# Buffers of a cross-interaction recommender kernel declared in another order: index, embedding and bias buffers last in SBUF

## The reference

```python
def _cin_layer(x0, xk, W, b):
    out = jnp.einsum('bhd,bmd,shm->bsd', xk, x0, W) + b[None, :, None]
    return jax.nn.relu(out)
e  = jnp.stack([tbl_f[ids[:, f]] for f in range(39)], axis=1)   # [1024, 39, 16]
x1 = _cin_layer(e, e, W1, b1)                                   # [1024, 128, 16]
x2 = _cin_layer(e, x1, W2, b2)                                  # [1024, 128, 16]
h = jnp.concatenate([x1.sum(-1), x2.sum(-1), dense_ctx], axis=1)  # [1024, 272]
h = jnp.maximum(h @ W_top1 + b_top1, 0.0)
h = jnp.maximum(h @ W_top2 + b_top2, 0.0)
y = h @ W_top3                                                  # [1024, 1]
```

## Time and profile before

| | |
|---|---|
| median of 3 runs | 1221.91 us (1220.79 to 1225.9) |
| the profiled execution: its own time | 1218.08 us |
| its span, first to last instruction | 1216.3 us |
| mean granted TensorE clock in it | 0.992 |

### The profile page before, as it was taken

The page is one execution under the profiler, slowest core; times in us unless marked ns, Lnnn a source line. Parts: engine busy times, 40 slices in busy tenths (PEclk is TensorE's granted clock), DMA queues, the critical chain, the costliest instruction groups (busy, mean ns, idle before and its releaser), DMA issues.

```text
span 1216.3 us, 17500 instructions
## 1 busy us (share of the span) xinstructions
PE 1130.8 (93%) x4468; PEld 829.6 (68%) x4468; DVE 941.1 (77%) x2846; ACT 801.2 (66%) x2718; POOL 847.9 (70%) x956
## 2 busy tenths in 40 slices
PE   0069999999999999999999999999999999999996
PEld 0037777777777777777776567777777777776685
DVE  2027878889898888888887468998888889875786
ACT  4017767777777767777776467777776777765683
POOL 7745878788678878778787466788777864542455
PEclk9999999999999999999999999999999999999997
DMA  5256568675876477665976248764686748652341
GB/s 167 46 124 142 106 127 178 127 150 103 177 164 126 93 149 170 137 131 100 202 139 139 46 81 178 163 137 82 146 174 122 141 99 200 148 129 44 71 92 33
DMA packets 73516, 154.47 MB, mean 127 GB/s; under 512 B 14339, under 2 KB 27525, under 8 KB 73414
## 3 DMA queue, kind: packets, MB, share of 16 engines
q0 software_dynamic: 28272, 85.81, 39.5%
q1 hardware_dynamic: 45142, 67.53, 21.0%
HBM read 66.26 MB, written 3.81 MB: 58 GB/s over the span
## 4 chain that ended last, share of the span: by engine, by line
PE 58%; issue 15%; POOL 14%; DMA 8%; DVE 2%; ACT 1%; SPq 1%; another core or an unknown queue 1%; POOLq 0%; DVEq 0%; ACTq 0%
PE bank L604 46%; PE l_acc L588 10%; DMA prod<-prod 6%; POOL tree L306 4%; POOL emb L277 2%; POOL tree L313 2%; POOL prod L288 2%; POOL tree L318 1%; POOL a_sum L327 1%; DVE acc L506 1%; DMA z<-e_rows 1%; ACT prod L394 1%; PE misc L624 1%; PE misc L627 1%
## 5 line engine op out<-in xcount | busy, mean ns | idle before, releaser
L394 ACT ACTIVATE prod<-bank,emb 128x128 f32<-128x128 f32 x2560 | 724.7, 376 | 329.3 <-PE bank L604 299.5
L506 DVE SCALAR_TENSOR_TENSOR acc<-bank,emb,acc 128x128 f32<-128x128 f32 x2176 | 612.5, 342 | 154.7 <-PE bank L604 133.6
L604 PE MATMUL bank<-w2h,x1h 128*128 128x512 f32 (+1 forms) x1280 | 542.3, 424 | 8.2 <-DVE acc L506 4.5
L604 PE MATMUL bank<-w2l,x1h 128*128 128x512 f32 (+1 forms) x1280 | 498.1, 389 | 0.0
L604 PE MATMUL bank<-w2h,x1l 128*128 128x512 f32 (+1 forms) x1280 | 475.5, 434 | 2.0 <-issue 1.5
L277 POOL DMA_INDIRECT emb<-tbl,idx x312 | 311.2, 997 | 82.2 <-issue 76.0
L604 PEld LDWEIGHTS bank<-w2h,x1h 128*128 128x128 f32 x1280 | 241.2, 188 | 113.2 <-issue 58.5
L306 POOL TENSOR_TENSOR tree<-prod 128x640 f32<-128x640 f32 x128 | 241.7, 1888 | 91.2 <-DMA prod<-prod 91.1
L604 PEld LDWEIGHTS bank<-w2h,x1l 128*128 128x128 f32 x1280 | 240.9, 188 | 92.8 <-issue 37.2
L604 PEld LDWEIGHTS bank<-w2l,x1h 128*128 128x128 f32 x1280 | 241.6, 189 | 67.9 <-issue 23.3
L288 POOL DMA_DIRECT2D prod<-prod x127 | 125.1, 985 | 184.8 <-ACT prod L394 182.0
(11 more groups left out here) (79 smaller groups left out, 291.3 us busy)
## 6 DMA issues: line engine op xcount, KB each, us to landing
prod<-prod POOLq DMA_DIRECT2D x127, 640.0 KB
z<-e_rows SPq DMA_DIRECT2D x160, 234.0 KB
z<-e_rows SPq DMA_DIRECT2D x192, 78.0 KB
emb<-tbl,idx POOLq DMA_INDIRECT x312
z<-e_rows SPq DMA_DIRECT2D x32, 156.0 KB
prod<-w_by_h SPq DMA_DIRECT2D x3, 832.0 KB
e_rows<-e_t SPq DMA_DIRECT2D x8, 256.0 KB
wt<-w_top SPq DMA_DIRECT2D x2, 512.0 KB
```

The costliest lines, as they stand in the source:

```text
L394: last = nc.scalar.activation(prod[:, ct % P_RING, i, n * S:(n + 1) * S], bank[:, (ct * NB + k) % RING, n * S:(n + 1) * S], ACT.Copy, scal ...
L506: nc.vector.scalar_tensor_tensor(dst, src, scale, dst if step else b2_row[:, :], ALU.mult, ALU.add).then_inc(v_step, 1)
L604: last = nc.tensor.matmul(out_bank[:, 0:b - a], x, w[:, a:b], start=(n == 0), stop=(n == 2))
```

## The change

Six declarations are moved behind the others; nothing else differs, and each engine has the same instructions in the same order.

```diff
         wt2 = sb("wt2", [P, N1 // P, N2])
-        wt3 = sb("wt3", [P, N2 // P])
-        bias1 = sb("bias1", [P, 1])
         b2_row = sb("b2_row", [P, S])
-        biast1 = sb("biast1", [P, N1 // P])
-        biast2 = sb("biast2", [P, N2 // P])
         ident_f = sb("ident_f", [P, P])
         ctx_t = sb("ctx_t", [P, B])
-        idx = sb("idx", [P, TILES, M], I32)
-
-        emb = sb("emb", [P, E_SLOTS, M * D])
+
         e_t = sb("e_t", [P, 5, P])
...
         y = sb("y", [1, B])
+
+        emb = sb("emb", [P, E_SLOTS, M * D])
+        idx = sb("idx", [P, TILES, M], I32)
+        biast1 = sb("biast1", [P, N1 // P])
+        wt3 = sb("wt3", [P, N2 // P])
+        biast2 = sb("biast2", [P, N2 // P])
+        bias1 = sb("bias1", [P, 1])
```

## The result

The changed kernel takes 1212.99 us (median of 6 runs, 1210.79 to 1215.25) against 1222.29 us of the kernel before (6 runs, 1220.34 to 1225.9): 9.3 us faster, ratio 0.9921, interval 0.9903 to 0.9938. The forecast was no change at 1221.9 us, and its range ended at 1213.5.

The account below looks back on a forecast made before the run. TensorE was taken to bound the kernel: 78.0 us of start, 1117.7 at its pace, 20.6 of tail and 0 for the change gave 1216.3 us of span, forecast as a 1221.9 us median, range 1213.5 to 1229.6.

Parts of the forecast that it names:

- the sign that was named for being wrong: Time from first to last layer-2 matmul, forecast within 2 us of 1117.7; moving over 6 us would refute the forecast.
- B: Layer-2 matmul step shortens by 0.002 us as stationary operands leave offset 32: 7.7 us faster, 1214.2 us; chance 0.13.
- D: Buffers at equal offsets modulo 2048 delay each other, lengthening TensorE's step by 0.002 us: 7.7 us slower, 1229.6; chance 0.09.
- item 2: TensorE's moving operands (`w2h`, `w2l`, `z`): taken as 0; far ends 15.7 us slower for `z`, 77 us faster in layer 2.
- Item 1: TensorE's weight loads of `x1h` and `x1l`: 188 ns, the same as aligned `wt2` loads, so 0.
- the far end: Fast-side limit: all 0.020 us of layer-2 step excess due to `x1h` and `x1l` at offset 32, 77 us to win.
- Items 3 to 6: VectorE and ScalarE operations, GpSimd, gathers, SBUF transfers: each taken as 0; GpSimd's tail kept at -1.4 to +1.4 us.
- rival C: GpSimd's additions shorten by up to 22%, only the tail gains: 1.4 us faster, 1220.5 us; chance 0.08.

Follow-up runs that it names:

- e5: Changed kernel with `w2h`, `w2l` and `w1` moved to 32 bytes past a multiple of 64, all others still at multiples of 64; ratio 1.0005 to the kernel before.
- e10: Kernel before with `w2h`, `w2l` and `w1` also moved to 32 bytes past a multiple of 64, like `x1h` and `x1l`; ratio 0.9945.

## Why the prediction was wrong

**What bounds the kernel.** Right in the main: TensorE's step sets the time, and it is TensorE's busy time that fell. A step shorter by 3 to 4 ns moved the end by 9.3 us. That a gain "passes straight to the end" until VectorE's 919 us bound the stretch was too simple: VectorE has slack over the stretch but not in its merges, and waits there took part of the gain back. Because of such waits, and because the profiled execution of before lay 4.2 us under its median, the sign that was named for being wrong, a middle stretch moved by over 6 us, didn't show in the single traces (2.0 us). The nine-matmul step, where B and D were to show, did.

**The step that failed** is in item 2: "I take 0, because the weight loads, which alone touch `x1h` and `x1l`, are equal by the row and not on the path." The loads are indeed equal, 188 ns in both the earlier trace rows, and the step changed nevertheless, from 15.03 to 14.75 us for 66. A load starts together with the previous matmul, as here in the kernel before:

```profile
600.37 0.40 PE L604 MATMUL bank<-w2l,x1h 128*128 128x512 f32 x1
600.37 0.19 PEld L604 LDWEIGHTS bank<-w2h,x1h 128*128 128x128 f32 x1
```

Its own duration didn't show what the pair costs. That the cost comes from both reading SBUF at the same time is a guess that fits e5 and e10; no run tests it. Item 1's zero rested on the same pair of rows. The excess of 0.020 us a step, which I had named as the far end, was in fact partly this: some 4 ns of the 20, and the sum had it at 0.

**Item 2, `z`.** Right at zero: the contraction took 0.86 us at offsets 32/0 (`z`, `w1`), 0/0 and, in e5, 0/32; from the second load of a contraction to the next layer-2 load it is a median of 432 ns in all three. These fp32 matmuls don't show the effect. The 15.7 us on the slow side, from `ctx_t` against `p1`, were the shape's, as suspected: 640 and 604 ns now, both aligned.

**Items 3 to 6.** Right. The durations of the operations costed there didn't move: 692 and 680 for `w2l` and `x1l`, 613 and 588 for ScalarE's casts, and GpSimd's five additions after the last bank still take 6.4 us. So rival C was wrong. The 2% on in-place additions was asked of rows that couldn't show it; the packets' 409 ns before and 413 after are 1%, and on the time it was nothing that can be seen, as said.

**Rival B** was the mechanism as far as place and sign go, an excess of the layer-2 step due to where its stationary operand lies. It was priced at 2 ns, an arbitrary tenth of the excess, with 3 to 4 measured, and given 0.13; that its 1214.2 us lies so near to 1212.99 is partly luck, since waits took back some of the larger step gain. What it had wrong is that an address 32 off costs by itself: against a moving operand also 32 off it costs nothing (e10).

**Rival D** had the pair right and the sign wrong. Equal offsets of 0 or of 32 don't delay each other; unequal ones do. What was held against it, that `w2l` and `w2h` lie at different places modulo 2048 and run alike, was blind to this, since modulo 64 they are the same.

**The Trainium skill's** lines of 16 bytes (SBUF — State Buffer, Specifications) gave zero for every engine; the runs show a difference between offsets of 0 and 32, both multiples of 16. The measurement decides: the page's figure is not enough to call such a change free.

## What to carry to other kernels

Where `float32r` matmuls with a new stationary operand each follow each other without a gap, as here, let the stationary and the moving buffer both begin at a multiple of 64 bytes; the simplest way is to declare odd-sized buffers last. An equal offset of 32 did as well, one of 16 didn't. It is worth some 4 ns of 230 a matmul here and takes no instruction; other engines' waits can take part of it back. The equal duration of an operation that is hidden doesn't show that it is free for the one beside it, so price the step of the pair.

## What the runs showed of the hardware

- A layer-2 step depends on the offsets of both operands modulo 64: 66 matmuls took 14.75 us at 0/0, 15.04 at 32/0 and at 0/32, 14.89 at 16/0 and 14.97 at 16/16 (stationary/moving); nine took 2.06 at 32/32, as at 0/0.
- Weight loads took 188 or 189 ns in all of these.
- With one of two stationary buffers aligned, 66 matmuls took 14.98 us (`x1h`) and 15.08 (`x1l`); with both aligned the whole gain came.
- The fp32 contraction took 0.86 us whether its operands' offsets were equal or not.
- The packets of the in-place additions, 5120 bytes each, had a median of 404 ns where `prod` began at a multiple of 256, 409 at 32 and 64 past one, and 411 to 414 at 96 to 192.
